# Small-head attention: turned scores go pair by pair over key tiles 0 and 1, masks and values of tile 0 a step later

## The chip, the cores and the metric

One core of a Trainium2 chip runs the whole program in one launch. The metric is the device time in microseconds; the kernel before takes 1814.21 us (median of three executions, 1813.55 to 1821.56). The profile is of one further execution.

## The reference

The model is two "macaron" layers on x of shape (2, 512, 512): a layer is half a feed-forward, an attention and half a feed-forward, each behind a layer norm and added to x. Only layer 0's attention is touched. It has 32 small heads of 16 columns, rotary embedding and a causal mask, and beside it each query looks at ten adapter tokens:

```
scores = q @ k.T / sqrt(16);  scores = where(causal, scores, -inf)
y = softmax(scores) @ v
y = y + gating * softmax(q @ ak.T / sqrt(512)) @ av
out = y.transpose @ w_proj.T
```

## The kernel before

The attention of layer 0 has three blocks: one makes q, k and v with the rotation, `heads_block` computes the heads, and a third projects. The change lies in `heads_block` alone.

**Units.** A group is 8 heads of one batch row; a unit is half of a group, four heads, and there are NU = 16 units. A unit has two pairs of heads, `ab` = 0 and 1; the two heads of a pair lie in rows 0 to 63 and 64 to 127 of the transposed tiles `qt` and `kt`, each head with its high and low halves and two further rows for a shift. `pipeline` calls `turn` once per unit on each engine, for n from -3 to NU + 1. Within a turn, work of unit n (`d` = 0) is mixed with preparation of units n+1 to n+3 and the end of units n-1 to n-3. `half()` tells the first and the second unit of a group: adapter scores (`adapter_scores`, 16 matmuls of 20 columns, step 2) and `final` (step 0, from unit 3 on) run in odd units, `adapter_turn` (step 1) in even ones.

**What happens to one pair.** GpSimd spreads q and k into `qe` and `ke` (`expand`), TensorE transposes them into the PSUM bank `prep` (`turn_pair`, L1711), and ScalarE copies that to `qt` and `kt` (L1860). One bank `prep` serves all transposes, so each waits for the copy of the one before. TensorE computes plain scores (`scores`, L1722), and VectorE takes the maxima of rows (`maxes`, L2024), two instructions behind one another in two score banks. GpSimd splits the negated maxima (`split`, L1946, L1948), TensorE transposes them (`shift_turn`, L1729), ScalarE copies them to `xrow` (`shift_copy`, L1866), and SP issues four small DMAs (`shift`, L1691) that write them as the shift rows of `qt`.

**The step loop.** Each turn has six steps, `two` = 0 to 5. Step `two` computes "turned" scores, keys down and queries across, of unit n (`crossed`): before the change steps 0 and 1 take key tile 0 for pair 0 and 1, steps 2 and 3 key tile 1 for pair 0 and 1 (L1741), step 4 tile 2 and step 5 tile 3 for both pairs (L1746). They are 512, 384, 256 and 128 queries wide. They go round three PSUM banks `across`, ScalarE takes their exponential into the SBUF array `slabs` (`exps`, L1879), and `exp_ready` counts 12 exps per unit. When all exps of a key tile are done, which `ENDS` counts, GpSimd clears the part over the diagonal (`keep`, L1954), and TensorE multiplies by the values (`values`, L1758). Tile 0 is done at step 3, tile 1 at step 5, tiles 2 and 3 at steps 0 and 1 of the next turn. ScalarE copies the sum out at step 2 (`out_copy`, L1884), TensorE turns it to tokens at step 4 (`tokens`, L1769) and VectorE normalises it.

**Order and waits.** Each engine runs its instructions in the order in which they are written; nothing is planned by the program. TensorE's step is: `crossed`, two `scores`, then what the step number adds (a transpose, `values`, and so on). The waits which matter are `shift_loaded[ab]` before pair `ab` is first read in `crossed`; `exp_ready` for the bank `across` three uses back; `copied` and `shift_copied` for the bank `prep`; `maxed` for the score banks; `kept` before `values`; `pv_done` of the unit before in front of `exps`, since `slabs` has one buffer; `ot_copied` before the values of tile 0.

On GpSimd a turn is: keep tile 3 of the unit before, split pair 0, expand two, in even units the product `aprob` (L1974), keep tile 0, split pair 1, expand, keep tile 1, expand, keep tile 2, then the smaller ones.

Of the kernel before, what the change touches and what calls it, by code (L numbers as in the profile page):

```python
# [88 lines left out]
def wait(eng, sem, count):  # L89

    if not (isinstance(count, int) and count <= 0):
        eng.wait_ge(sem, count)
# [1488 lines left out]
def heads_block(nc, env, dram, name, q, k, v, ak, av):  # L1581
# [8 lines left out]
    SL = 4  # L1590
    XROW = 3 * HD0
    WIDE = [T - kn * P for kn in range(TB)]
    ENDS = [4, 8, 10, 12]
    MAXED = [2, 4, 5, 6, 7, 8]
    NAG = TB * GH
    PLACE = [0, 2, 1, 3]
    with ExitStack() as ctx:
# [80 lines left out]
        with nc.Block() as block:  # L1678
# [23 lines left out]
            def _(pe):  # L1702
                def turn_pair(u, d, ab, which):
                    m = u.pair(d, ab)
                    src = (qe, ke)[which][ab]
                    wait(pe, built, 6 * m + 3 + 3 * which)
                    wait(pe, copied, 2 * m + which)
                    if which == 0:
                        wait(pe, shift_copied, m - 2)
                    for t in range(TB):  # L1710
                        last = pe.transpose(prep[:, t * P:(t + 1) * P], src[:, t, :, :, :].rearrange("p h s d -> p (h s d)").bitcast(F32), ident[:, :])  # L1711
                    last.then_inc(turned, 1)
# [17 lines left out]

                def crossed(u, two):

                    kn = 0 if two < 2 else 1 if two < 4 else two - 2
                    if two < 2:
                        wait(pe, shift_loaded[two], 64 * (u.unit() + 1))
                    w = WIDE[kn]
                    for n in range(2):
                        wait(pe, exp_ready, 12 * u.unit() + 2 * two + n - 2)
                        if kn < 2:
                            ab = two % 2  # L1740
                            pe.matmul(across[(2 * two + n) % 3][:, 0:w], kt[rows(n), u.slot(0, ab), kn * P:(kn + 1) * P],  # L1741
                                      qt[rows(n), u.slot(0, ab), kn * P:T], start=True, stop=True).then_inc(across_ready, 1)
                    if kn >= 2:
                        for ab in range(2):
                            for n in range(2):
                                last = pe.matmul(across[(2 * two + n) % 3][:, ab * w:ab * w + w], kt[rows(n), u.slot(0, ab), kn * P:(kn + 1) * P],  # L1746
                                                 qt[rows(n), u.slot(0, ab), kn * P:T], start=True, stop=True)
                                if ab == 1:
                                    last.then_inc(across_ready, 1)

                def values(u, d, kn):
                    wait(pe, kept, 4 * u.unit(d) + kn + 1)
                    if kn == 0:
                        wait(pe, vz_ones, 2)
                        wait(pe, vz_built, u.group(d) + 1)
                        wait(pe, ot_copied, u.unit(d))
                    for h in range(HU):
                        last = pe.matmul(outp[32 * h:32 * h + 32, kn * P:T], vz[u.buf(d)][:, kn, u.half(d) * HU + h, :], slab(kn)[:, PLACE[h], :],  # L1758
                                         start=kn == 0, stop=kn == TB - 1)
                    last.then_inc(pv_done, 1)  # L1760
# [41 lines left out]
                def turn(u):  # L1802
                    for two in range(6):
                        ab, use = ((1, 2 * two) if two < 3 else (0, 2 * two - 6))
                        d = 1 if two < 3 else 2
                        if u.has():
                            crossed(u, two)
                        if u.has(d):
                            scores(u, d, ab, use)
                            scores(u, d, ab, use + 1)  # L1810
                        if two == 0:
                            if u.has(2):
                                turn_pair(u, 2, 0, 0)
                            if u.has(-1):
                                values(u, -1, 2)
                            if u.half() and u.has(-3):
                                final(u)
                        if two == 1:
                            if u.has(2):
                                turn_pair(u, 2, 0, 1)  # L1820
                            if u.has(-1):
                                values(u, -1, 3)
                            if not u.half() and u.has(-2):
                                adapter_turn(u)
                        if two == 2:
                            if u.has(1):
                                shift_turn(u, 0)
                            if u.half() and u.has():
                                adapter_scores(u)
                        if two == 3:  # L1830
                            if u.has(2):
                                turn_pair(u, 2, 1, 0)
                            if u.has():
                                values(u, 0, 0)
                        if two == 4:
                            if u.has(2):
                                turn_pair(u, 2, 1, 1)
                            if u.has(-1):
                                tokens(u)
                        if two == 5:  # L1840
                            if u.has(1):
                                shift_turn(u, 1)
                            if u.has():
                                values(u, 0, 1)
# [11 lines left out]
            def _(act):  # L1856
# [9 lines left out]
                    act.activation(xrow[ab][:, :], prep[0:16, 0:P], ACT.Copy, scale=-1.0).then_inc(shift_copied, 1)  # L1866

                def exps(u, two):
                    kn = 0 if two < 2 else 1 if two < 4 else two - 2
                    wait(act, pv_done, 4 * u.unit(-1) + kn + 1)  # L1870
                    w = WIDE[kn]
                    for n in range(2):
                        use = 2 * two + n
                        wait(act, across_ready, 12 * u.unit() + use + 1)
                        if kn < 2:
                            dst, src = slab(kn)[:, 2 * n + two % 2, :], across[use % 3][:, 0:w]
                        else:
                            dst, src = slab(kn)[:, 2 * n:2 * n + 2, :], across[use % 3][:, 0:2 * w].rearrange("p (h w) -> p h w", h=2)
                        act.activation(dst, src, ACT.Exp).then_inc(exp_ready, 1)  # L1879
# [49 lines left out]
            def _(pool):  # L1929
# [32 lines left out]
                def turn(u):  # L1962
                    if u.has(-1):
                        keep(u, -1, 3)
                    if u.has(1):
                        split(u, 0)
                    if u.has(2):
                        expand(u, 2, 1, 0)
                        expand(u, 2, 1, 1)
                    if not u.half() and u.has(-2):  # L1970
                        n = u.group(-2)
                        wait(pool, inverse_ready, n + 1)
                        wait(pool, apt_ready, n)
                        pool.tensor_tensor(aprob[:, :, :], asub[:, :, :], spread(ainv[:, :], [P, NAG, AK]), ALU.mult).then_inc(aprob_ready, 1)  # L1974
                    if u.has():
                        keep(u, 0, 0)
                    if u.has(1):
                        split(u, 1)
                    if u.has(3):
                        expand(u, 3, 0, 0)  # L1980
                    if u.has():
                        keep(u, 0, 1)
                    if u.has(3):
                        expand(u, 3, 0, 1)
                    if u.has():
                        keep(u, 0, 2)
                    if u.half() and u.has(1):
                        value_tiles(u)
                    if u.half() and u.has():
                        n = u.group()  # L1990
                        wait(pool, out_ready, n)
                        pool.tensor_tensor(avb[:, :], av[:, bass.ds(n // B, 1), :].rearrange("p a f -> p (a f)"), gatemask[:, :], ALU.mult).then_inc(avb_built, 1)
                    if not u.half() and u.has():
                        n = u.group()
                        wait(pool, ascore_ready, n)
                        pool.tensor_copy(akt[:, :, :].rearrange("p a n -> p (a n)"), akt_all[:, bass.ds(n // B, 1), :].rearrange("p a n -> p (a n)")).then_inc(akt_built, 1)
# [214 lines left out]
```

## Time and profile before

| | |
|---|---|
| median of three | 1814.21 us |
| the profiled execution | 1815.23 us |
| its span | 1813.5 us |
| busy over the span | PE 89%, PEld 69%, DVE 54%, ACT 50%, POOL 55% |
| `heads_block` | about 163 to 430 us of the span |
| units 0, 8, 15 begin (first turned score) | 190.57, 310.21, 411.67 us |

PE is TensorE's matmuls, PEld its weight loads, DVE VectorE, ACT ScalarE, POOL GpSimd. The end of a matmul is modelled, so starts are the safer numbers; a start-to-start distance is what an instruction costs in a row of others.

### The profile page before, as it was taken

To read this page: it belongs to the slowest core of one execution; us is meant where nothing else is said; L and a number is where in the kernel's file an instruction comes from. 1 tells how busy PE (TensorE), PEld (TensorE's weight loads), DVE (VectorE), ACT (ScalarE), POOL (GpSimd) and SP (SyncE) were. 2 spreads that over 40 slices of the span, in tenths; PEclk is the share of its full clock that TensorE was granted. 3 is DMA by queue.
4 is the path that set the end of the run, shared out by engine and by line. 5 is a ranking of instruction groups with operands and counts; after the bars stand their busy time and mean duration, and the time that the engine had idled before them with its cause. 6 is when DMAs were issued, how large, how long until landed. Compare 5 with 4: busy or idle time off the path is not lost. (4 is left out here: it accounts for less than half of the span.)

```text
span 1813.5 us, 26474 instructions
## 1 busy us (share of the span) xinstructions
PE 1620.5 (89%) x8164; PEld 1242.8 (69%) x8164; DVE 986.8 (54%) x2614; ACT 902.2 (50%) x1876; POOL 1001.3 (55%) x1138
## 2 busy tenths in 40 slices
PE   5697899998769998589999999999999999979996
PEld 4486555545547886467878788787878778757884
DVE  5561555552656236655556565655555555565235
ACT  2112555652221231477677777767677776731230
POOL 2252455541221443478787877878788776812533
PEclk9798798988879999899999999999999999989998
DMA  2200000000133933344454353443534344463834
GB/s 84 95 5 3 2 3 2 3 3 1 37 141 151 345 129 105 96 102 105 115 106 114 79 139 84 104 116 93 123 88 125 80 96 91 87 227 124 315 123 133
DMA packets 312096, 180.24 MB, mean 99 GB/s; under 512 B 281895, under 2 KB 283767, under 8 KB 309568
## 3 DMA queue, kind: packets, MB, share of 16 engines
q1 hardware_dynamic: 300160, 152.81, 30.3%
q0 software_dynamic: 11840, 26.25, 4.6%
q8 instruction: 49, 0.80, 0.2%
q14 instruction: 47, 0.39, 0.1%
HBM read 111.08 MB, written 22.54 MB: 74 GB/s over the span
## 5 line engine op out<-in xcount | busy, mean ns | idle before, releaser
L1320 POOL TENSOR_TENSOR st_prob<-st_prob,st_rinv 128x512 f32<-128x512 f32 x256 | 269.0, 1052 | 170.9 <-DVE st_rinv L1382 170.9
L1324 POOL TENSOR_TENSOR st_plane<-st_prob,st_plane 128x512 f16<-128x512 f32 x256 | 306.3, 1207 | 0.3 <-ACT st_plane L1242 0.3
L1242 ACT ACTIVATE st_plane<-st_prob 128x512 f16<-128x512 f32 x256 | 161.2, 630 | 133.0 <-POOL st_prob L1320 132.9
L1258 ACT ACTIVATE st_prob<-st_score,st_nmax 128x512 f32<-128x512 f32 x256 | 175.2, 684 | 54.9 <-DVE st_nmax L1389 52.9
L1389 DVE TENSOR_REDUCE st_nmax<-st_score 128x1 f32<-128x512 f32 x256 | 175.0, 684 | 41.6 <-PE st_score L108 38.7
L2024 DVE CUSTOM_DVE_ANT_0 st1b_dump<-st1b_score,st1b_maskrow 128x128 f32<-128x128 f32 (+3 forms) x256 | 112.6, 486 | 98.0 <-PE st1b_score L1722 71.4
L1237 ACT ACTIVATE st_pthi<-st_plane_t 128x512 fp32r<-128x512 f16 x256 | 159.5, 623 | 3.3 <-DMA st_plane_t<-st_plane 3.2
L1367 DVE TENSOR_TENSOR st_olo<-st_outp,st_ohi 128x512 fp32r<-128x512 f32 x64 | 44.3, 692 | 203.6 <-ACT st_ohi L1246 203.6
L1363 DVE CAST st_ptlo<-st_plane_t 128x512 fp32r<-128x512 f16 x256 | 153.2, 599 | 2.4 <-DMA st_plane_t<-st_plane 2.3
L1879 ACT ACTIVATE st1b_slabs<-st1b_across 128x512 f32<-128x512 f32 (+1 forms) x192 | 90.6, 526 | 90.9 <-PE st1b_across L1741 69.3
L106 PE MATMUL st_outp<-st_pthi,st_vhi 128*128 128x512 f32 x256 | 105.1, 410 | 21.1 <-ACT st_pthi L1237 20.2
L742 POOL DMA_INDIRECT st_xg<-rows,st_source x62 | 62.8, 1013 | 109.2 <-DVE st_source L932 62.5
L614 PE MATMUL st_bank<-st_xts,st_raw 128*128 128x128 f32 x992 | 121.0, 275 | 0.7 <-ACT st_xts L707 0.7
L614 PEld LDWEIGHTS st_bank<-st_xts,st_raw 128*128 128x128 f32 x992 | 115.8, 192 | 2.1 <-issue 2.1
L835 DVE COPY st_ln_xn<-st_bank 128x512 f32<-128x512 f32 x62 | 42.9, 692 | 130.9 <-PE st_bank L621 121.2
L106 PE MATMUL st_sbank<-st_owhi,st_ohi 128*128 128x512 f32 x240 | 97.2, 405 | 9.6 <-POOL st_owlo L1314 9.0
L106 PE MATMUL st_score<-st_khi,st_qhi 128*128 128x512 f32 x256 | 101.2, 395 | 3.7 <-DVE st_qlo L1350 2.6
L108 PE MATMUL st_outp<-st_pthi,st_vlo 128*128 128x512 f32 x256 | 104.1, 407 | 0.0
L107 PE MATMUL st_outp<-st_ptlo,st_vhi 128*128 128x512 f32 x256 | 103.5, 404 | 0.0
L108 PE MATMUL st_qbank<-all_xhi,st_qwlo 128*128 128x512 f32 x256 | 100.0, 390 | 0.0
L107 PE MATMUL st_score<-st_klo,st_qhi 128*128 128x512 f32 x256 | 99.7, 389 | 0.0
L108 PE MATMUL st_score<-st_khi,st_qlo 128*128 128x512 f32 x256 | 99.7, 389 | 0.0
(379 smaller groups left out, 4062.4 us busy)
## 6 DMA issues: line engine op xcount, KB each, us to landing
st_raw<-in_moe_w SPq DMA_DIRECT2D x40, 768.0 KB, 8.0
sorted_outs<-st_ln_xn SPq DMA_DIRECT2D x62, 256.0 KB, 3.1
st_qraw<-in_gqa_q SPq DMA_DIRECT2D x8, 1024.0 KB, 5.3
st_oraw<-in_gqa_o SPq DMA_DIRECT2D x8, 1024.0 KB, 5.2
rows<-st_ln_xn SPq DMA_DIRECT2D x2, 2048.0 KB, 9.3
st_kvraw<-in_gqa_kv SPq DMA_DIRECT2D x8, 512.0 KB, 3.9
st_plane_t<-st_plane SPq DMA_TRANSPOSE x256, 2.8
st1a_raw<-in_w_attn SPq DMA_DIRECT2D x3, 1024.0 KB, 5.5
```

The costliest lines, as they stand in the source:

```text
L106: pe.matmul(out, w_hi, m_hi, start=first, stop=False)
L107: pe.matmul(out, w_hi, m_lo, start=False, stop=False)
L108: return pe.matmul(out, w_lo, m_hi, start=False, stop=last)
L614: last = pe.matmul(out[:, 0:P], part(raw[w % RAW], k, which), xts[n % 2][:, k * P:(k + 1) * P], start=k == 0, stop=k == KC - 1)
L1237: act.activation(pthi[:, :, t * P:(t + 1) * P], plane_t[t][:, 0:TB, :], ACT.Copy).then_inc(pthi_ready, 1)
L1242: act.activation(plane[t][:, 0:T], prob[:, t, :], ACT.Copy).then_inc(upper_ready, 1)
L1258: act.activation(prob[:, t, :], score[t][:, :], ACT.Exp, bias=nmax[:, slot:slot + 1], accum_out=rsum[:, slot:slot + 1]).then_inc(exp_ready, 1)
L1320: pool.tensor_tensor(prob[:, t, :], prob[:, t, :], rinv[:, slot:slot + 1].broadcast_to([P, T]), ALU.mult).then_inc(norm_ready, 1)
L1324: pool.tensor_tensor(plane[t][:, T:2 * T], prob[:, t, :], plane[t][:, 0:T], ALU.subtract).then_inc(lower_ready, 1)
L1363: dve.tensor_copy(ptlo[:, :, t * P:(t + 1) * P], plane_t[t][:, TB:2 * TB, :]).then_inc(ptlo_ready, 1)
L1389: dve.tensor_reduce(nmax[:, slot:slot + 1], score[t][:, :], AX, ALU.max, negate=True).then_inc(nmax_ready, 1)
L2024: dve.tensor_tensor_reduce(dump[done % 2][:, 0:w], score[use % 2][:, at:at + w], maskrow[:, T - w:T], 1.0, -3e38, ALU.add, ALU.max, nmx[ab ...
```

## The change

The pair and the tile change places in the first four steps: steps 0 and 1 now take pair 0 on key tiles 0 and 1, steps 2 and 3 pair 1 on key tiles 0 and 1. So pair 1 and its shift rows are first read at step 2. Key tile 0 is complete after exp 6 of the unit in place of exp 4. TensorE's values of tile 0 go from step 3 to step 4, behind the transpose of `ke` and ahead of `tokens`. GpSimd's mask of tile 0 goes behind the split of pair 1 and the expand of q of unit n+3.

```diff
-    ENDS = [4, 8, 10, 12]
+    ENDS = [6, 8, 10, 12]
@@ TensorE, crossed
-                    kn = 0 if two < 2 else 1 if two < 4 else two - 2
-                    if two < 2:
-                        wait(pe, shift_loaded[two], 64 * (u.unit() + 1))
+                    kn, ab = (two % 2, two // 2) if two < 4 else (two - 2, None)
+                    if two in (0, 2):
+                        wait(pe, shift_loaded[ab], 64 * (u.unit() + 1))
@@
-                            ab = two % 2
@@ TensorE, turn
                         if two == 3:
                             if u.has(2):
                                 turn_pair(u, 2, 1, 0)
-                            if u.has():
-                                values(u, 0, 0)
                         if two == 4:
                             if u.has(2):
                                 turn_pair(u, 2, 1, 1)
+                            if u.has():
+                                values(u, 0, 0)
                             if u.has(-1):
                                 tokens(u)
@@ ScalarE, exps
-                    kn = 0 if two < 2 else 1 if two < 4 else two - 2
+                    kn, ab = (two % 2, two // 2) if two < 4 else (two - 2, None)
@@
-                            dst, src = slab(kn)[:, 2 * n + two % 2, :], across[use % 3][:, 0:w]
+                            dst, src = slab(kn)[:, 2 * n + ab, :], across[use % 3][:, 0:w]
@@ GpSimd, turn
-                    if u.has():
-                        keep(u, 0, 0)
                     if u.has(1):
                         split(u, 1)
                     if u.has(3):
                         expand(u, 3, 0, 0)
+                    if u.has():
+                        keep(u, 0, 0)
                     if u.has():
                         keep(u, 0, 1)
```

## Rows read from the trace of the kernel before

**Rows 1.** TensorE's waits, 180 to 435 us: total us, times, longest.
```profile
PE st1b_across L1741 <- DMA st1b_qt<-st1b_xrow: 14.1, 9, 2.2
```
**Rows 2.** Busy by stretch (stage, units 6, 8, 9, 11): PE, PEld, DVE, ACT, POOL, clock.
```profile
199.00:429.00 230.00, 211.05 (x1520) 120.92 (x1519) 125.21 (x517) 133.84 (x308) 110.90 (x306) 0.88 0.01 2
279.54:294.42 14.88, 12.52 (x94) 7.03 (x90) 8.51 (x38) 8.83 (x20) 7.98 (x23) 0.89 0.01 3
310.21:322.89 12.68, 11.09 (x94) 6.20 (x91) 8.48 (x38) 8.71 (x20) 7.96 (x23) 1.00 0.02 4
322.89:338.86 15.97, 15.64 (x116) 9.26 (x113) 9.19 (x38) 9.03 (x21) 7.40 (x23) 0.89 0.01 3
351.47:368.95 17.48, 17.16 (x117) 10.58 (x114) 9.18 (x38) 9.07 (x21) 7.61 (x23) 0.80 0.01 1
```
**Rows 3.** TensorE's timeline, even unit 8: start, us, what, idle before.
```profile
311.51 0.64 PE L1758 MATMUL st1b_outp<-st1b_slabs,st1b_vz 128*32 128x256 f32 x8
...
313.55 0.50 PE L1741 MATMUL st1b_across<-st1b_qt,st1b_kt 64*128 64x512 f32 x2 [1.40 <-DMA st1b_qt<-st1b_xrow]
...
315.72 0.45 PE L1741 MATMUL st1b_across<-st1b_qt,st1b_kt 64*128 64x384 f32 x2
...
317.89 0.63 PE L1711 MATMUL st1b_prep<-all_ident,st1b_qe 128*128 128x128 f32 x4 [0.19 <-POOL st1b_qe L1938]
318.45 1.06 PE L1758 MATMUL st1b_outp<-st1b_slabs,st1b_vz 128*32 128x512 f32 x8
319.45 0.51 PE L1746 MATMUL st1b_across<-st1b_qt,st1b_kt 64*128 64x256 f32 x4
...
320.12 0.66 PE L1711 MATMUL st1b_prep<-all_ident,st1b_ke 128*128 128x128 f32 x4
320.62 0.60 PE L1769 MATMUL st1b_misc<-all_ident,st1b_ot 128*128 128x128 f32 x4
...
321.42 0.55 PE L1722 MATMUL st1b_score<-st1b_kt,st1b_qt 64*128 64x256 f32 x2
321.90 0.28 PE L1729 MATMUL st1b_prep<-all_ident,st1b_nsp 128*16 128x128 f32 x1
```
**Rows 4.** ScalarE's timeline, even unit 8.
```profile
309.75 0.25 ACT L1866 ACTIVATE st1b_xrow<-st1b_prep 16x128 fp32r<-16x128 f32 x1
310.80 1.09 ACT L1879 ACTIVATE st1b_slabs<-st1b_across 128x512 f32<-128x512 f32 x2 [0.80 <-PE st1b_across L1741]
...
316.26 0.87 ACT L1879 ACTIVATE st1b_slabs<-st1b_across 128x384 f32<-128x384 f32 x2 [0.54 <-PE st1b_across L1741]
317.02 0.60 ACT L1884 ACTIVATE st1b_ot<-st1b_outp 128x512 f32<-128x512 f32 x1
317.50 0.25 ACT L1866 ACTIVATE st1b_xrow<-st1b_prep 16x128 fp32r<-16x128 f32 x1
...
318.13 0.83 ACT L1879 ACTIVATE st1b_slabs<-st1b_across 128x384 f32<-128x384 f32 x2
318.88 0.57 ACT L1860 ACTIVATE st1b_qt<-st1b_prep 128x512 fp32r<-128x512 f32 x1
```
**Rows 5.** VectorE's timeline, even unit 8, steps 3 and 4.
```profile
317.56 0.29 DVE L2024 CUSTOM_DVE_ANT_0 st1b_dump<-st1b_score,st1b_maskrow 128x128 f32<-128x128 f32 x1 [0.46 <-POOL st1b_nsp L1946]
...
318.47 0.55 DVE L2024 CUSTOM_DVE_ANT_0 st1b_dump<-st1b_score,st1b_maskrow 128x384 f32<-128x384 f32 x1
...
320.84 0.69 DVE L2024 CUSTOM_DVE_ANT_0 st1b_dump<-st1b_score,st1b_maskrow 128x512 f32<-128x512 f32 x1
```
**Rows 6.** GpSimd's timeline, even unit 8.
```profile
312.74 0.73 POOL L1974 TENSOR_TENSOR st1b_aprob<-st1b_asub,st1b_ainv 128x320 f32<-128x320 f32 x1
...
318.08 0.46 POOL L1940 TENSOR_TENSOR st1b_qe<-st_q,st1b_qe 128x128 fp32r<-128x128 f32 x1
```
**Rows 7.** TensorE's timeline, odd unit 7, step 3.
```profile
303.20 0.44 PE L1741 MATMUL st1b_across<-st1b_qt,st1b_kt 64*128 64x384 f32 x2
...
304.44 1.63 PE L1758 MATMUL st1b_outp<-st1b_slabs,st1b_vz 128*32 128x512 f32 x8
```

## The prediction

> **What bounds the kernel now.** I read the page first (the stage of the small heads lies in slices 4 to 10), then the windows of that stage, then TensorE's waits in it, then the timelines of one even and one odd unit. Over the 230 us from 199 to 429 TensorE is busy 211.05, the others at most 133.84 [rows 2]. What TensorE waits for there is nearly all one thing: 14.1 us in 9 waits, at most 2.2, for the DMAs that write the shift rows into qt [rows 1]. In starting order of units they are 1.52 (unit 0), 1.66 (1), 1.18 (2), 1.65 (4), 2.24 (6), 1.40 (8), 1.34 (10), 1.18 (12), 1.93 (14); the row of unit 8 stands in [rows 3]. They sit at step 1, where pair 1 of the unit is first read. The odd units from 3 on have none: `final` lies in their step 0 and covers the landing. So the bound is TensorE's own work, plus this wait in the even units. ScalarE, VectorE and GpSimd have slack on average, but short chains through them follow TensorE closely within a unit, and what the change is worth is decided there.
>
> **Part 1: pair order in steps 1 and 2.** Nothing is added or removed; the number and shapes of the matmuls and exps are the same. Pair 1 is first read at step 2. In unit 8, TensorE is free at 313.55 - 1.40 = 312.15 (the values of the unit before end there [rows 3]). Now pair 0 on key tile 1 starts then. The shift rows of pair 1 had landed by 313.55, 3.80 us after their copy began at 309.75 [rows 4]. Step 2 started 2.17 after step 1 (315.72 against 313.55), so it would now start at 312.15 + 2.17 - 0.05 = 314.27 (the matmul of step 1 is narrower, 384 for 512 columns, 0.45 for 0.50 us). That is 0.7 after the landing: the whole wait is covered, and step 2 starts 1.45 earlier. Call its start C.
>
> Then ScalarE is late. Step 2's two exps are now 512 wide in place of 384. From [rows 4], a wide one costs 0.49 start to start (1.09 for two, less the 0.60 that one activation of this shape lasts), a narrow one 0.38 (two from 316.26 to 317.02); the first exp starts 0.59 after its matmul (310.21 to 310.80) for 0.54. So out_copy and the xrow copy, next on ScalarE, move 0.27 later from C. TensorE's transpose of qe in step 3 stood at C + 2.17 (317.89), right behind the xrow copy that frees the bank prep; it comes at C + 2.44.
>
> **Part 2: values of tile 0 go from step 3 to step 4.** They took 1.00 us of TensorE (318.45 to 319.45) between that transpose and step 4's scores, and hid two ScalarE steps. Without them step 4's scores are wanted at C + 2.44 + 0.56 = 3.00, but need step 3's first exp: the xrow copy starts at C + 2.05, the exps 0.63 behind it, the first lasts 0.87 - 0.38 = 0.49, so C + 3.2. The transpose of ke in step 4 would come 0.67 later, at 3.9, and needs the qt copy (0.75 after step 3's exps begin, 0.57 long), so C + 4.1. Then 0.50 of transposes, the values (1.00), and tokens at C + 5.60; they stood at C + 4.90 (320.62). Part 2 loses 0.70 from C in an even unit. It gives something back: at step 5 the second score matmul waits for VectorE, whose last 512-wide maximum ran from 320.84 to 321.53 [rows 5]. The 1.00 us of values now lie in between, the 0.48 from 321.42 to the shift transpose at 321.90 becomes about the 0.21 of the same scores in step 2: 0.27 won.
>
> **Part 3: keep(0,0) behind split and expand on GpSimd.** It has margin. expand of qe ends at 318.08 + 0.46 [rows 6], which is C + 2.82 counted from 315.72; the mask takes 0.64; tile 0 is kept at C + 3.5, and its values start at C + 4.6. split and expand are no longer behind an exp. What else is queued on GpSimd, the next keep, needs exps that end at C + 3.6 anyway: cost nothing. But aprob, which ended at 312.74 + 0.73 = 313.47 [rows 6], was hidden by the DMA wait; the adapter transposes would now be wanted at 313.7, 0.2 after it, and step 5 before is 0.27 shorter: I charge 0.15 per even unit. SP's queue issues the same eight DMAs per unit in the same order, and loses nothing. ScalarE's wait on pv_done for tile 1 moves one step up, but TensorE has issued those values before step 1's scores, so it is met in order.
>
> **Sum, even unit:** wait w gone, -w - 0.05, +0.70, -0.27, +0.15 = -(w - 0.5). For unit 8, 0.9 of its 12.68 us.
>
> **Odd units.** The adapter scores between steps 2 and 3 hide ScalarE's longer step 2. In steps 3 and 4 it depends on the clock. In unit 7 TensorE ran this part at full clock: step 3 at X = 303.20, values at X + 1.24 [rows 7]. Step 4's scores would then be wanted at X + 1.6 and need VectorE to finish step 3's four maxima, which take 1.46 (317.56 to 319.02 [rows 5]) from about X + 0.95: X + 2.5 for the second, and the ke transpose 0.2 later where 1.9 was possible. That is 0.8 lost, less 0.27 in step 5, and less 0.1 to 0.2 in step 2, where exps narrower by 0.22 in step 1 free the bank earlier. So +0.4. Where this part runs at half clock (five of the six odd units from 3 to 13, by the longer matmuls in the timeline; units 9 and 11 have granted clocks of 0.89 and 0.80 [rows 2]), TensorE is slower than these chains and only the small gain of step 2 stands, -0.1. Together with the last unit, which has no transposes to cover the moved values (about +0.6), the odd units give +0.8. Unit 1 has no final and keeps 1.66 - 0.2.
>
> **Total.** Waits 14.1; less 8 x 0.5 (even) = 4.0, less 0.2, less 0.8: 9.1 us. To this I add 0.6 for the clock. Unit 6, with the longest wait, has a granted clock of 0.89 and lasts 14.88 us against 12.68 of unit 8 at 1.00: 2.20 more, of which the wait is 0.84, so 1.4 come from half clock [rows 2]. With the wait gone this stretch goes with a chance of nearly a half. 9.7 us in all. The profiled execution was 1815.23 us (span 1813.5 and 1.7 around it), so 1805.5 for it; it lies 1.0 above the median 1814.21, so 1804.5 for the median. No other stage is touched.
>
> TensorE's granted clock fell to its lower level (1.2 of 2.4 GHz) in the odd units behind the adapter scores, 16 matmuls of 20 columns, and in even ones only where the wait was longest [rows 2]. The Trainium skill, page "TensorE: Matmul & The Clock Gate", section "Part 1: The HAM clock gate (the "warmup" mystery)", says that the default state is throttled and activity releases the throttle; the trace agrees. By that rule filling 14 us of idle would win more than the wait itself, and moving 1 us of values away from behind the adapter scores could lose it again.
>
> **Rivals.**
> R1, the chains take the place of the wait. If exps, copies and maxima follow TensorE as closely everywhere as in steps 3 and 4 of unit 8, an even unit gives back 1.0 to 1.4 and each odd one loses the full 0.8. Gain 14.1 - 8 x 1.1 - 7 x 0.4 = 2.5 up to 5: 1809 to 1812. For it: unit 8's margins computed above are 0.2 to 0.7 us. Against: each engine's sum in that unit is at most 8.71 of 12.68 besides TensorE [rows 2].
> R2, more full clock. The even units stay at 1.00 and three odd units shrink from the long form to the short (unit 11 is 17.48 us, unit 9 is 15.97: 1.5 each [rows 2]): 9.1 + 1.4 + 1.4 (unit 14) + 3 x 1.5 = 16, so 1798. For it: idle is removed. Against: the adapter scores, behind which the clock falls, remain.
> R3, slower. The waits of Part 2 lie now in steps 3 and 4, right behind the adapter scores, and new short ones in every even unit. If by this the three short odd units (7, 9, 13) go the long form (+1.5 each, 4.5) and the five even units at full clock lose a stretch (+1.4 each, 7), 9.1 of gain turn into 2.4 of loss: 1816.6; with R1's losses beside it, 1822. It decides from about six added stretches of half clock. Against: the even units kept 1.00 with waits of 1.2 to 1.65 in one piece, which are longer than any of the new ones.
> Bounds: below, all waits gone, none of the chains' costs, and R2, 1796; above, R3 with R1, 1822. I take the middle since unit 8's rows give each term.
>
> **Numbers.** About 0.5% (9.07 us) is what a measurement of this kernel can tell from no change; below 1805.1 is faster. Forecast 0.56, from 1801 to 1809, 0.33 of it below 1805.1; R1 0.20; R2 0.17; R3 0.07, 0.06 of it over 1823 or from what I have not seen. Faster 0.50, same 0.44, slower 0.06. The range is 1798.5 to 1811.5.
>
> **What would show it.** In the profile after: no wait of TensorE for the DMA into qt, or under 1 us in all (right); otherwise the landing was not covered. Unit 8's like at 11.6 to 12.0 us. New short waits of step 4's scores for the exps, and of the ke transpose for ScalarE's qt copy, 0.2 each, in even units; second score of step 4 for VectorE in full-clock odd units. Values of tile 0 never waiting for the mask (if they do, Part 3 is wrong). The transpose of qe 2.4 behind step 2's scores. Wrong would be: even units no shorter than 12.5, or a granted clock over the stage below 0.85 or above 0.92, for 0.88 now.

## The result, and the profile after

The changed kernel takes 1819.81 us (median of 22 executions, 1812.69 to 1823.64) against 1812.91 for the kernel before (22, 1805.8 to 1821.56): ratio 1.0037, interval [1.0024, 1.005]. Forecast was 1804.5 with a range up to 1811.5. It became 7 us slower, not 10 us faster. The profiled execution is 1817.51 us, span 1815.8.

The wait that the change aims at is gone, as forecast. TensorE's waits from 180 to 435 us (total, times, longest), which answer to [rows 1], hold no DMA:

```profile
PE st1b_across L1745 <- ACT st1b_slabs L1878: 3.6, 8, 1.6
PE st1b_prep L1711 <- POOL st1b_qe L1937: 2.4, 6, 0.4
PE st1b_score L1722 <- DVE st1b_nmx L2023: 1.4, 5, 0.6
```

Yet TensorE is busy for 220 us of the same 230, with no more matmuls than before: each takes longer. The busy times by stretch, for the stage, even unit 6 and odd unit 9, answer to [rows 2]; the granted clock is the number behind POOL's, and 0.84 is below the 0.85 that the prediction had named as a sign of being wrong:

```profile
199.00:429.00 230.00, 220.09 (x1483) 120.70 (x1482) 123.71 (x513) 132.61 (x304) 108.95 (x306) 0.84 0.01 2
283.74:296.08 12.34, 11.49 (x94) 6.11 (x90) 8.25 (x36) 8.67 (x20) 7.41 (x23) 1.00 0.01 3
327.28:345.54 18.26, 18.14 (x116) 10.11 (x112) 9.81 (x40) 9.15 (x21) 8.57 (x26) 0.78 0.01 2
```

The clock has two levels, so a mean of 0.84 means half clock for 2 x 0.16 x 230 = 74 us; before it was 55. From unit 0 to unit 15 the stage takes 225.53 us (191.96 to 417.49); before 221.10. The odd unit 9 is 18.26 us where it was 15.97. From unit 3 to 13 the odd units last 17.58 to 18.27 us (15.78 to 17.48 before). Over the 22 executions of the changed kernel time and the granted clock of the whole span (0.933 to 0.941) go together with a correlation of -0.85, 1.15 us for each 0.001.

Where the fall of the clock lies is seen on TensorE's timeline of odd unit 7, which answers to [rows 7]. The 20-column adapter scores end at 304.6; the transposes of qe at 305.25 are at full clock (0.66 us for four), those of ke at 307.69 at half (1.11), and the values of tile 0 take 1.94 us in place of 1.06:

```profile
302.73 1.92 PE L1779 MATMUL st1b_misc<-st1b_akt,st1b_qt 128*128 128x20 f32 x16
304.59 0.44 PE L1740 MATMUL st1b_across<-st1b_qt,st1b_kt 64*128 64x384 f32 x2
...
305.25 0.66 PE L1711 MATMUL st1b_prep<-all_ident,st1b_qe 128*128 128x128 f32 x4
305.83 0.50 PE L1745 MATMUL st1b_across<-st1b_qt,st1b_kt 64*128 64x256 f32 x4
306.28 0.49 PE L1722 MATMUL st1b_score<-st1b_kt,st1b_qt 64*128 64x512 f32 x1
306.97 0.79 PE L1722 MATMUL st1b_score<-st1b_kt,st1b_qt 64*128 64x512 f32 x1 [0.20 <-DVE st1b_nmx L2023]
307.69 1.11 PE L1711 MATMUL st1b_prep<-all_ident,st1b_ke 128*128 128x128 f32 x4
308.73 1.94 PE L1757 MATMUL st1b_outp<-st1b_slabs,st1b_vz 128*32 128x512 f32 x8
310.60 1.12 PE L1768 MATMUL st1b_misc<-all_ident,st1b_ot 128*128 128x128 f32 x4
```

At full clock the order itself runs as worked out. TensorE's timeline of even unit 8 from step 2 on (C = 319.48) answers to [rows 3]: the qe transpose at C + 2.44 (forecast 2.44), step 4's scores at C + 3.28 (3.2), the ke transpose at C + 4.13 (4.1), tokens at C + 5.69 (5.60). The engine named beside the first wait is the last by the profile; that transpose also needs the bank, which ScalarE's xrow copy frees.

```profile
319.48 0.51 PE L1740 MATMUL st1b_across<-st1b_qt,st1b_kt 64*128 64x512 f32 x2
...
321.92 0.63 PE L1711 MATMUL st1b_prep<-all_ident,st1b_qe 128*128 128x128 f32 x4 [0.40 <-POOL st1b_qe L1937]
322.76 0.50 PE L1745 MATMUL st1b_across<-st1b_qt,st1b_kt 64*128 64x256 f32 x4 [0.22 <-ACT st1b_slabs L1878]
...
323.61 0.63 PE L1711 MATMUL st1b_prep<-all_ident,st1b_ke 128*128 128x128 f32 x4
324.17 1.07 PE L1757 MATMUL st1b_outp<-st1b_slabs,st1b_vz 128*32 128x512 f32 x8
325.17 0.66 PE L1768 MATMUL st1b_misc<-all_ident,st1b_ot 128*128 128x128 f32 x4
```

### The profile page after: what moved, and what is told of

It reads as the page before. It is cut to its first block and busy times, and to the rows that moved or that the text cites. A ratio compares the mean times of both kernels' runs of the same rounds, so it can differ in the third digit from the quotient of the medians.

```text
span 1815.8 us, 26475 instructions
## 1 busy us (share of the span) xinstructions
PE 1631.7 (90%) x8164; PEld 1242.0 (68%) x8164; DVE 986.7 (54%) x2614; ACT 902.2 (50%) x1876; POOL 999.5 (55%) x1138
## 5 line engine op out<-in xcount | busy, mean ns | idle before, releaser
L1878 ACT ACTIVATE st1b_slabs<-st1b_across 128x512 f32<-128x512 f32 x192 | 90.3, 523 | 85.5 <-PE st1b_across L1740 53.2
```

## The experiments

All ratios are to the kernel before on the same chip, with 95% intervals. "Clock" is the granted clock from 199 to 429 us of the profiled execution (before 0.88, changed 0.84). It is a figure of one execution: a second profile of the changed kernel (e18) gives 0.82. The mean clock of the whole span is on record for every execution, and is given where it matters.

**e1 and e2: one half of the change each.** e1 keeps the new pair order, but leaves TensorE's values and GpSimd's mask of tile 0 where they were:

```diff
                         if two == 3: ...
+                            if u.has():
+                                values(u, 0, 0)
                         if two == 4: ...
-                            if u.has():
-                                values(u, 0, 0)
```

> The changed kernel with the values of tile 0 back at step 3 and their mask back at its old place on GpSimd; only the pair order of steps 1 and 2 is changed. Theory A (the dense values moved away from behind the adapter scores let the clock fall for longer): TensorE's DMA waits stay gone, the half-clock stretches of odd units return to the 3 to 7 us they had, granted clock over the stage at 0.88 or more, and only the 0.27 us of ScalarE per even unit is lost: 9 to 13 us faster than the kernel before, about 1802. Theory B (a shorter, regular group period, whatever fills it, makes the clock fall longer): half-clock stretches of about 10 us per group remain, time within 5 us of the changed kernel. Theory C (short waits on ScalarE and VectorE eat the gain): 3 to 8 us faster than before, with those waits in the list.

Measured: 1797.23 us, 0.9924 [0.9897, 0.9951], clock 0.91. This is what theory A gave. In the windows of e1 (stage, even unit 6, odd unit 7) the even unit lasts 11.83, what was forecast for the changed kernel, and the odd one 15.71:

```profile
199.00:429.00 230.00, 220.08 (x1571) 129.52 (x1568) 127.13 (x516) 134.07 (x306) 107.64 (x300) 0.91 0.01 2
272.23:284.06 11.83, 11.38 (x96) 6.29 (x92) 8.32 (x37) 8.80 (x20) 7.93 (x23) 1.00 0.02 3
284.06:299.77 15.71, 15.59 (x118) 9.37 (x114) 9.18 (x38) 9.02 (x21) 7.34 (x23) 0.89 0.01 2
```

TensorE's timeline of that odd unit shows that the clock still falls behind the adapter scores (half clock at 293.25), but is back at full by 297.00. TensorE idles 0.12 us in this unit (15.71 less 15.59), and just as much in odd unit 9 of the changed kernel (18.26 less 18.14): the longer time at half clock does not come with more idle time.

```profile
290.72 1.92 PE L1779 MATMUL st1b_misc<-st1b_akt,st1b_qt 128*128 128x20 f32 x16
...
293.25 1.11 PE L1711 MATMUL st1b_prep<-all_ident,st1b_qe 128*128 128x128 f32 x4
294.30 1.94 PE L1757 MATMUL st1b_outp<-st1b_slabs,st1b_vz 128*32 128x512 f32 x8
...
297.00 0.66 PE L1711 MATMUL st1b_prep<-all_ident,st1b_ke 128*128 128x128 f32 x4
```

e2 is the other half: the kernel before with the values moved to step 4 and the mask moved.

> The kernel before with only the values of tile 0 moved to step 4 and their mask moved on GpSimd; the pair order is the old one. Theory A: DMA waits of 14 us remain, half-clock stretches grow to about 10 us in the odd groups, clock over the stage near 0.85: 6 to 12 us slower than before. Theory B: stretches as before, time +0 to +5 us. Theory C: even units 0.4 to 0.7 us longer by the waits for the exp and the qt copy, at an unchanged clock: +5 to +8 us.

Measured: 1828.52 us, 1.0099 [1.0071, 1.0127], more than any theory gave. Clock 0.83, so 78 us at half clock against 55, up to 12 us; the rest is left for the opened waits, of which a new one for ScalarE shows in TensorE's waits beside the DMA wait, which stays. The windows are those of the stage and of an odd unit (15.97 and 17.48 in [rows 2]):

```profile
PE st1b_across L1741 <- DMA st1b_qt<-st1b_xrow: 11.9, 8, 2.7
PE st1b_across L1746 <- ACT st1b_slabs L1879: 2.1, 6, 1.0
```
```profile
199.00:429.00 230.00, 214.92 (x1442) 121.56 (x1441) 121.80 (x510) 128.08 (x294) 107.03 (x303) 0.83 0.01 2
333.27:351.08 17.81, 17.48 (x117) 10.21 (x113) 9.13 (x38) 9.21 (x21) 7.93 (x23) 0.81 0.01 2
```

The halves nearly add up: -13 and +18 make +5, the whole measured +7. The move of tile 0's values and mask is the cause of the loss. Not all of e1's 13 us are the wait: its clock is 0.91 for 0.88, 41 us at half clock for 55, which is worth up to 7.

**e5: mask or values?** The changed kernel with only GpSimd's `keep(u, 0, 0)` back ahead of split and expand.

> The changed kernel with only the mask of tile 0 back at its old place on GpSimd; the values stay at step 4. By my working of GpSimd the mask had margin, so theory A (the move of TensorE's values is the cause) expects the time of the changed kernel, 1.002 to 1.006 of the kernel before, and the same long half-clock stretches. If the mask's move is a cause, it is 5 us or more faster than the changed kernel.

Measured: 1821.78 us, 1.0058 [1.0039, 1.0077], clock 0.85. With the values at step 4 the mask's place makes no difference that the intervals can tell. e5 and e1 (0.9924) differ in nothing but the place of TensorE's values, so it is the values that matter.

**e3 and e4: without the light work.** In both orders one matmul of 320 columns takes the place of the sixteen of 20 columns. The adapter scores themselves are left out of these two kernels.

```diff
-                    for t in range(TB):
-                        for p in range(PAIRS):
-                            last = pe.matmul(misc[:, at:at + 2 * AK], qt[...], akt[:, p, :], ...)
+                    last = pe.matmul(misc[:, 0:NAG * AK], kt[:, u.slot(0, 0), 0:P], qt[:, u.slot(0, 0), 0:NAG * AK], ...)
```

> The kernel before with the 16 adapter score matmuls of 20 columns of each odd unit replaced by one matmul of 320 columns into the same bank (the adapter scores themselves are left out). Theory A and B: the half-clock stretches of the odd units vanish nearly, clock over the stage 0.95 or more. It saves 8 x 1.6 us of matmuls and up to 15 us of clock: 20 to 28 us faster than before. The DMA waits stay or grow (no change in step 0). If the clock falls for another reason, the stretches remain and it is 10 to 13 us faster.

> The changed kernel with the same replacement of the adapter scores (left out). If the loss lies in the clock behind the adapter scores alone (A, B), this is 7 to 10 us faster than the kernel before with the same replacement: the gain that was forecast for the changed kernel comes out. If the chains of ScalarE, VectorE and GpSimd are the cause (C), it is within 3 us of it or slower, since these waits are not hidden by the adapter scores any more.

Measured: e3 1790.34 us, 0.9893 [0.9865, 0.9921], clock 0.95; e4 1782.85 us, 0.9849 [0.9822, 0.9876], clock 0.97. The changed order is now 7.5 us ahead by the medians (the two intervals just overlap). With the adapter scores gone, so are nearly all falls of the clock: they are what it falls behind. But the gain is not what I had worked out per unit, as the windows of one even and one odd unit of each show, all at full clock, e3 first:

```profile
353.49:366.04 12.55, 11.08 (x95) 6.20 (x92) 8.28 (x37) 8.71 (x20) 8.06 (x23) 1.00 0.01 3
366.04:379.10 13.06, 12.73 (x101) 7.29 (x97) 9.16 (x38) 8.99 (x21) 5.66 (x17) 1.00 0.01 2
```
```profile
318.43:330.84 12.41, 11.50 (x94) 6.11 (x90) 8.28 (x37) 8.67 (x20) 7.64 (x23) 1.00 0.01 3
330.84:344.32 13.48, 13.11 (x101) 7.27 (x97) 9.08 (x38) 9.03 (x21) 7.67 (x23) 1.00 0.01 3
```

The odd unit loses 0.42 (0.4 was forecast for full clock, but with the adapter scores as cover in step 2, which are not there now). The even one wins 0.14, not 0.7 to 0.9: at full clock the new order is level with the old one. e4 met its forecast of 7 to 10 us for another reason than the one given. In the profiled pair, whose spans are 5.5 us apart, the difference lies in the first two units: from unit 0 to unit 2 e3 takes 31.33 us (191.34 to 222.67) and e4 25.59 (189.26 to 214.85). There the early units' DMA waits lie, and the granted clock is 0.64 in e3 and 0.76 in e4.

**e7 and e6: where the light work stands.** e7 is the changed kernel with `adapter_scores(u)` moved from step 2 to step 3, behind the transpose of qe. e6 is e1 with the adapter scores in two halves, query tiles 0 and 1 at step 2, tiles 2 and 3 at step 3.

> The changed kernel with all of its adapter scores moved from step 2 to step 3, behind the transpose of qe. They cover the waits of step 4 for VectorE and ScalarE in odd units (0.8 us each by my working), but step 3 then follows step 2 with ScalarE's chain open (0.3). The dense values of tile 0 stand 2 us closer behind them. Theory A: half-clock stretches of 3 to 7 us in place of 7 to 10, 5 to 12 us faster than the changed kernel: 0.997 to 1.0 of the kernel before. Theory C (only the waits count): 3 to 4 us faster than the changed kernel at an unchanged granted clock.

> e1_pairs_only (pair order changed, values and mask at their old places) with the adapter scores in two halves: 8 matmuls of 20 columns at step 2 as now, 8 at step 3 behind the transpose of qe and ahead of the values. The same work in total. Theory A (it is light work standing together that lets the clock fall): the one stretch of 3.4 us per group goes in most groups, up to 1.5 us each, 1785 to 1793 for 1797 of e1, clock over the stage 0.95 or more. If the light work counts by its sum over a group, not by how closely it stands, the stretches stay and it is within 3 us of e1.

Measured: e7 1804.33 us, 0.996 [0.9937, 0.9982], clock 0.90, about 15 us under the changed kernel, a little more than theory A gave and far more than C: with the adapter scores and the values closer together again, most of the loss by the clock is gone. e6 1795.38 us, 0.9921 [0.989, 0.9952], clock 0.91, the time of e1. Splitting the light work changes nothing, where theory A had expected 1785 to 1793 and 0.95: that it is the light work standing together that counts is not borne out.

**e8 and e11: add work.** In the changed kernel step 4's four matmuls of turned scores are issued four times (e8) or twice (e11) in the odd units, with the same result:

```diff
-                        for ab in range(2):
+                        for at, ab in enumerate((0, 1) * (4 if kn == 2 and u.half() else 1)):
```

> The changed kernel with step 4's four matmuls of turned scores issued four times in the odd units, into the same bank with the same result: 12 more matmuls of 256 columns in each of 8 units, about 1.0 us of dense work each at full clock, at the place where TensorE waits for VectorE. Only work is added. Theory A (the clock falls since dense work is missing behind the adapter scores): the long stretches shrink by one of 3.4 us in most groups, granted clock over the stage 0.87 or more for 0.84, and the time is 2 to 8 us less than the changed kernel's. If missing work is not the cause, it is 2 to 8 us more.

> The changed kernel with step 4's four matmuls issued twice in the odd units, four more of 256 columns (about 0.35 us) in place of twelve. Theory A in degrees: between the changed kernel and e8 (1800), 1803 to 1815, the stretches per group 3.4 to 6.8 us for 6.8 to 10.2. If e8 gained by something else than the amount of dense work (a shift of phase), it may lie anywhere from 1798 to 1822.

Measured: e8 1799.99 us, 0.9941 [0.9922, 0.996], clock 0.95; e11 1806.1 us, 0.9979 [0.9963, 0.9995], clock 0.87. With 96 matmuls more the kernel is 17 us faster by the ratios (20 by the medians), the clearest sign that it is the clock that was lost. The profiled execution of e11, with 0.87, took 1812.50 us, 6 more than its median. In e8's windows (stage and an odd unit) that unit takes 15.01 us at full clock, against 18.26 above; its timeline has the sixteen matmuls and no wait for VectorE behind them:

```profile
199.00:429.00 230.00, 215.64 (x1655) 128.99 (x1655) 126.09 (x516) 134.17 (x307) 109.22 (x304) 0.95 0.01 3
229.84:244.85 15.01, 14.89 (x130) 9.56 (x126) 9.09 (x38) 9.10 (x21) 7.75 (x23) 1.00 0.01 3
```
```profile
239.59 1.21 PE L1745 MATMUL st1b_across<-st1b_qt,st1b_kt 64*128 64x256 f32 x16
240.64 0.58 PE L1722 MATMUL st1b_score<-st1b_kt,st1b_qt 64*128 64x512 f32 x2
```

**e9 to e17: the same in the other orders, elsewhere, and with another kind of work.** e9 and e10 are e8's addition in e1 and in the kernel before.

> e1_pairs_only with step 4's four matmuls of turned scores issued four times in the odd units, as in e8. Theory A (dense work behind the adapter scores keeps the clock): the one 3.4 us stretch per group goes in most groups (1.5 us each of 7), against 1.0 us of added matmuls each that nothing hides here: 1791 to 1799, about the time of e1 (1797 against 1810), with a granted clock over the stage of 0.95 or more. If the stretches of e1 have another cause, it is 6 to 8 us slower than e1.

> The kernel before with the same twelve more matmuls in each odd unit; it has the values of tile 0 in step 3 already. Theory A: its stretches of 3.4 to 6.8 us per group (51 us in the stage) shrink to under 30 us, worth up to 10 us, less 8 us of added matmuls: 0.995 to 1.0 of the kernel before. If dense work is lacking only in the changed order, the stretches stay and it is 6 to 8 us slower than before.

Theory A had expected e9 at 1791 to 1799 us and e10 at 0.995 to 1.0. They took 1805.2 and 1823.64 us, each longer than the kernel without the addition, so theory A as it stood (dense work behind the adapter scores keeps the clock, in any order) had failed, and I asked whether the place decides. e12 to e14 issue step 3's two matmuls of turned scores four times (`for _ in range(4 if two == 3 and u.half() else 1)`):

> e1_pairs_only with step 3's two matmuls of turned scores (384 columns) issued four times in the odd units, directly behind the adapter scores: six more in each of 8 units, about 1.0 us. Theory D (dense work keeps the clock only if it comes ahead of the point where the clock falls): the stretch per group goes in most groups, 1790 to 1798, under e9 (1805) by 7 us or more, clock over the stage 0.95 or more. Theory E (only the changed order with the values at step 4 can be repaired, by whatever e8 does): as e9, 1803 to 1808, clock 0.91.

> The kernel before with the same addition at step 3 of the odd units. Theory D: half-clock stretches shrink from 51 us to under 30, 0.993 to 1.0 of the kernel before, and 10 us or more under e10. Theory E: as e10, 1.004 to 1.008.

> The changed kernel with the same addition at step 3 of the odd units. Both theories expect it to win against the changed kernel (1820); D expects about e8's time, 1798 to 1804, since here step 4 is still ahead of the fall of the clock.

Or whether the kind of work does: e15 to e17 issue step 3's four transposes of qe three times.

> The changed kernel with step 3's four transposes of qe issued three times in the odd units, eight more of 128 columns over all 128 rows, 1.1 us at full clock. Theory F (the kind of work that the values are, over all rows, keeps the clock): few stretches, granted clock over the stage 0.92 or more, 1796 to 1804. If any added work does as well, about e14's 1810.

> The kernel before with the same addition. Theory F: stretches under 25 us in the stage, 1803 to 1811 against 1811 before, 10 us or more under e13 (1821). If what is added does not matter, 1816 to 1824 as e10 and e13.

> e1_pairs_only with the same addition. Theory F: 1790 to 1798, as e1 or under it, at a granted clock of 0.95 or more over the stage. If what is added does not matter, 1801 to 1806 as e9 and e12, clock 0.91.

| added in odd units | changed order | e1's order | order before |
|---|---|---|---|
| nothing | 1.0037 [1.0024, 1.005], clock 0.84 | 0.9924, 0.91 | 1, 0.88 |
| turned scores, step 4 | e8 0.9941, 0.95 | e9 0.9972 [0.9955, 0.999], 0.91 | e10 1.0053 [1.0026, 1.008], 0.86 |
| turned scores, step 3 | e14 0.9995 [0.9979, 1.001], 0.90 | e12 0.9954 [0.9935, 0.9972], 0.91 | e13 1.0069 [1.0042, 1.0096], 0.90 |
| transposes, step 3 | e15 0.9957 [0.9939, 0.9976], 0.93 | e17 0.9945 [0.9922, 0.9969], 0.92 | e16 1.0017 [0.9998, 1.0036], 0.92 |

Each addition wins in the changed order (by the ratios 8 to 17 us). Where the values are at step 3 none pays: e9, e10 and e13 lose clearly, and e12, e17 and e16 are level with e1 and the kernel before, or lose a little, within the intervals. Theory D fails: e12 and e13 stand directly behind the adapter scores and win nothing. What theory E said would happen did, but it names no mechanism.

The transposes missed all three times that theory F gave (1806.01, 1816.18 and 1802.79 us). In the order before they do better than added turned scores: e16 is under e13 beyond the intervals, and the mean clock of the whole span has a median of 0.949 for 0.940 in e13. A part of this is not the odd units' doing. The edit also adds its transposes to the preparing turn ahead of unit 0, and in all three kernels the clock is back at full there some 14 us earlier: from 190 to 203 us it is 1.00 in e15 and 0.50 in the changed kernel, and unit 0 lasts 11.02 us for 14.04. So these rows do not show which kind of work holds the clock.

Why additions do not pay where the values are at step 3 is in part price: without opened waits, TensorE pays for each added microsecond, and in e1's order the clock gains little (0.91 or 0.92 for 0.91). In e13 the stage's 0.90 is misleading. Over its 7 executions the clock of the whole span has a median of 0.940, against 0.944 for the kernel before on that chip, so e13 has no clock gain to set against its added work. Why the clock does not rise there as it does in the changed order stays open.

**e18: the changed kernel again.**

> The changed kernel once more, on the same chip as e15 to e17: every theory expects 1.002 to 1.006 of the kernel before, with half-clock stretches of 7 to 10 us per group in the profile.

1821.56 us, 1.0039 [1.002, 1.0057], clock 0.82, that is 83 us at half clock. The loss repeats, and so does the clock.

## Why the prediction was wrong

**Part 1, the covered wait: right.** The DMA wait went from 14.1 us to none, and pair 1's shift rows were there in time. What this is worth alone is seen in e1's even units at full clock: 11.83 us for 12.68, so 0.85 of unit 8's 1.40. The rest of e1's 13 us is clock.

**"For unit 8, 0.9 of its 12.68 us": too large.** Even units at full clock (6 and 12) last 12.34, not 11.8. The parts from step 2 on came out within 0.1. What I left out lies before step 2: the DMA wait had also hidden VectorE's maxima of step 0, which stand behind the normalisation and the adapter sums of the unit before. In even unit 6 of the changed kernel the second score matmul of step 1 now waits for them; TensorE's row has 0.96 us for the two matmuls (0.40 in unit 8 before, at 313.89), and VectorE's row shows the maximum of that bank still under way:

```profile
285.89 0.96 PE L1722 MATMUL st1b_score<-st1b_kt,st1b_qt 64*128 64x512 f32 x2
```
```profile
285.73 0.56 DVE L2023 CUSTOM_DVE_ANT_0 st1b_dump<-st1b_score,st1b_maskrow 128x384 f32<-128x384 f32 x1
```

I had charged 0.15 for GpSimd's aprob at this place; the term was 0.5 and of another engine. It belongs to the pair order and not to the moved values: e1, without the DMA wait too, has 0.80 us for the same two matmuls (at 274.39). Step 5 gave back less as well: from tokens to the next unit 2.11 us (325.17 to 327.28) for 2.27 before (320.62 to 322.89), 0.16 and not 0.27.

**Part 3, the mask costs nothing: right**, as far as the intervals tell (e5).

**Odd units: wrong on the clock.** The +0.4 for waits at full clock has 0.42 beside it in e3 against e4, but those kernels lack the adapter scores that the forecast had as cover, so the number is met and the working is not shown. The step that failed is: "Where this part runs at half clock ... TensorE is slower than these chains and only the small gain of step 2 stands." It took the half-clock stretches of the kernel before as given. They grew, from 55 to 74 us in the stage: odd unit 9 went from 15.97 to 18.26, unit 11 from 17.48 to 17.59, and even units 2, 4, 8 and 10, at full clock before, now have 2.1 to 2.7 us at half clock each. That is rival R3 by its outcome and its price (1816.6 to 1822; measured 1819.8), to which I gave 0.07. Its cause was not the one that it named, the opened waits. Against it I had set that even units kept full clock through waits of 1.2 to 1.65 us, and idle time did not decide: the odd units from 3 on idle 0.12 to 0.32 us in the changed kernel, 0.32 or 0.33 before, and 0.12 in e1, which has the short stretches. What changed is which work follows the adapter scores: values, or a second round of turned scores.

**The sum as it came out,** for the profiled pair from unit 0 to unit 15: -14.1 for the waits; +8 x 1.0 in the even units, where 8 x 0.5 was forecast; +0.8 for the others, taken over from the forecast and not measured; and 19 us more at half clock, up to 9.5 where TensorE is the bound. Together +4.2, measured +4.4. With one term taken over and one an upper bound, that the two agree so closely is partly luck. The 0.6 us of clock that I had added as a gain had the wrong sign.

On the rule of the Trainium skill that I cited ("TensorE: Matmul & The Clock Gate", "Part 1: The HAM clock gate (the "warmup" mystery)", activity releases the throttle): e8 agrees, with more matmuls, a clock of 0.95 for 0.84, and 17 to 20 us less. e10 does not: the same addition in the order before gave 0.86 for 0.88. I had read from it two opposite effects and priced only the pleasant one. The busy share would not have told: it rose from 211.05 to 220.09 us of 230 while the clock fell.

## What to carry to other kernels

Where the granted clock falls in a stage, list what TensorE does right behind the light work and price a move of it with a clock of its own, not the clock of before: moving 1 us of values one step away cost 18 to 21 us (e2 against the kernel before, the changed kernel against e1), more than the 14 us of waits. If a change has two halves, ask whether one needs the other; here the new pair order did not need the values moved, and that version (e1, 0.9924) beats both kernels. A wait that disappears may have covered other waits at its own place: follow each engine's backlog to that point, not only from there on.

## What the runs showed of the hardware

- Issuing 96 redundant matmuls made a kernel 17 to 20 us faster (ratio 0.9941 for 1.0037, 1799.99 us for 1819.81), by the granted clock of the stage, 0.95 for 0.84. The same in the order before made it slower (e10, 1.0053).
- Replacing 16 matmuls of 20 columns by one of 320 in eight units raised that clock from 0.88 to 0.95 (e3) and from 0.84 to 0.97 (e4). Splitting the sixteen in two halves did nothing (0.91 in e1 and e6).
- The clock fell in units in which TensorE hardly idled: odd unit 9 of the changed kernel is busy 18.14 of 18.26 us at a mean clock of 0.78.
- One kernel's executions differ by 11 us (1812.69 to 1823.64), and most of this goes with the granted clock.
